# Latent attention of a six-block decoder on one core: lower context products with 66 stationary columns, each issued behind a turn

## The chip, the cores and the metric

The kernel runs on one core of one Trainium2 chip. The metric is device time in microseconds of a run. Lower is better.

## What is computed

The reference runs six blocks on x of 4 sequences x 256 tokens x 256 features, with a layer norm after each: sliding-window attention, cross attention to a context of 1601 rows x 64, a mixture of 8 experts, causal attention, the latent cross attention, and an attention with a second mixture of experts. The change lies in the fifth, the latent block. Per sequence b and head h (16 heads) it computes:

```
q_big = rope((hidden_q @ Wq.T) @ w_kc_q)
kv_r  = rope(kv_c)
scores = (q_big @ W_qr) . (kv_r @ W_kr)
attn  = softmax(scores)
ctx_c = attn @ kv_r
ctx   = ctx_c @ w_kc_kv.T
x    += ctx @ Wo.T
```

with kv_c the 1601 context rows. The kernel folds the weights of a head, so that a score is a product of the absorbed query with the roped context itself, and `ctx_c` is a 64-wide sum over 1601 rows.

## The kernel before

Most products are in two parts: a matrix is stored as an upper part rounded to fp32r and a lower part, the rest (names in `_hi` and `_lo`). `kvb[b]` holds for each of 13 tiles of 128 context rows the 64 features of `kv_r`: columns 0 to 63 the upper part, columns 64 to 127 the lower one. With that tile as the stationary operand, one product gives 128 rows: the sum over the upper part in rows 0 to 63, over the lower part in rows 64 to 127, and the weights of the output (`wf`) hold both halves.

`latent_attention` (L2427) goes through 64 units, one for each head and sequence. A unit consists of

- **absorb_q** (L2510), 6 products, after the query was projected (`project_q`, 12 products) and roped on POOL;
- **score** (L2521): for each half i of 128 queries, four pieces j of 304, 496, 496 and 305 context rows, in banks 0 to 3; two products each. A score waits until ACT's exponential has emptied the bank (`exped.at(s - 3)`, the piece four before it);
- **maximum** (L2692) on DVE, a reduction of each piece; after the fourth a small reduction, for which the exponential of the first piece waits;
- **exponential** (L2627) on ACT, with a read of the row sum, into `e_P`;
- **turn** (L2537) on PE: transposes of the probabilities, two tiles of context rows x two halves of queries in one of two banks; seven groups g (the last one has one tile of 65 rows), 26 transposes in a unit;
- **upper_pt** (L2641) on ACT, which copies the turned group to `e_PT_hi`, and **lower_pt** (L2709) on DVE, which takes the rest to `e_PT_lo`;
- **attend** (L2551) on PE: for each tile one product with `e_PT_hi` and one with `e_PT_lo`, all with the same stationary `kvb` tile, summed in one bank; 13 + 13 products in a unit. At g = 0 it waits for `cx_lo`, DVE's copy (L2717) of the previous unit's sum out of that bank;
- **project_out** (L2567), 6 products, and the addition to X on DVE.

All engines run the same loop of 8 steps for each unit (PE's at L2584), written out by hand, in the order of the code. While unit u is scored, unit u-1 is turned and summed: turn(v, step) at steps 0 to 6, attend(v, step-3) at steps 3 to 7 and attend(w, step+5), of the unit before, at steps 0 and 1. A step of PE is: four turns, up to four sums, one score of two products, then at step 1 absorb_q, at step 3 project_q, at step 5 the folding of a next head's weights, at step 7 project_out. A step of ACT is one exponential, copies for the step, upper_pt; of DVE one maximum and one lower_pt, with lower_context and lower_qk at step 2.

Of the kernel before, what the change touches and what calls it, by code (L numbers as in the profile page):

```python
# [16 lines left out]
P = 128  # L17
BATCH, SEQ, D = 4, 256, 256
TILES = BATCH * SEQ // P
DC = D // P  # L20
CTX, LAT = 1601, 64
# [33 lines left out]
def decoder(nc, t, out):  # L55
    with ExitStack() as top:
        pe, act, dve, pool, sp = nc.tensor, nc.scalar, nc.vector, nc.gpsimd, nc.sync
# [20 lines left out]
        bank = [psum[:, i, :] for i in range(8)]  # L78

        ident = vec("ident", [P, P])  # L80
# [18 lines left out]
        def mm(o, a, b, start, stop):  # L99
            return pe.matmul(o, a, b, start=start, stop=stop, skip_group_check=True)  # L100
# [2326 lines left out]
        def latent_attention(latent, before, following):  # L2427
            H, HALFQ = 16, latent.HALFQ
            LAG = 3
            PT_BUFS = LAG + 1  # L2430


            PIECES = (304, 496, 496, CTX - 1296)
# [2 lines left out]
            GROUPS = -(-KT // 2)  # L2436
            score_bank, tb_bank, ctx_bank, aux = (0, 1, 2, 3), (4, 5), 6, 7
# [5 lines left out]
            with ExitStack() as sc:  # L2443
# [27 lines left out]
                def keys_of(g):  # L2471

                    return min(2, KT - 2 * g), min(P, CTX - 2 * g * P)
# [12 lines left out]
                def tensor():  # L2486
                    free = [None]

                    def aux_bank():
                        if free[0]:  # L2490
                            pe.wait_ge(*free[0])
                        return bank[aux]

                    def fold_q(h):
                        latent.fold_q(h, aux_bank())
                        free[0] = wq_lo.at(h + 1)

                    def fold_r(h):
                        latent.fold_r(h, aux_bank())
                        free[0] = w2_lo.at(h + 1)  # L2500

                    def fold_o(h):
                        latent.fold_o(h, aux_bank())
                        free[0] = wf_lo.at(h + 1)

                    def project_q(m):
                        latent.project_q(m, aux_bank())
                        free[0] = q_kept.at(m + 1)

                    def absorb_q(m):  # L2510
                        h, z = m // BATCH, qr[m % 2]
                        pe.wait_ge(*z_lo.at(m + 1))
                        pe.wait_ge(*w2_lo.at(h + 1))
                        o = aux_bank()
                        for c in range(2):
                            last = mm3(o[:, 0:SEQ], [x[:, c, :] for x in w2[h % 2]], (z[0][:, c, :], z[1][:, c, :]),
                                       c == 0, c == 1)
                        last.then_inc(*q_absorbed.up())
                        free[0] = qk_lo.at(m + 1)

                    def score(u, i, j):  # L2521
                        s, k, o = 8 * u + 4 * i + j, qk[u % 2], bank[score_bank[j]]
                        if i == 0 and j == 0:
                            pe.wait_ge(*qk_lo.at(u + 1))
                            if u == 0:
                                pe.wait_ge(*latent.k_kept.at(latent.QUADS * BATCH + 1))
                                pe.wait_ge(*latent.padded.at(1))
                                pe.wait_ge(*q_kept.at(2))
                        if s >= 4:
                            pe.wait_ge(*exped.at(s - 3))  # L2530
                        size = PIECES[j] + PIECES[j] % 2
                        for n in range(2):
                            last = mm(o[:, 0:size], k[n][:, i * P:(i + 1) * P],
                                      KTb[:, u % BATCH, STARTS[j]:STARTS[j] + size], n == 0, n == 1)
                        last.then_inc(*scored.up())

                    def turn(u, g):  # L2537
                        at, p = GROUPS * u + g, Pm[u % 2]
                        o = bank[tb_bank[at % 2]]
                        n, rows = keys_of(g)  # L2540
                        pe.wait_ge(*exped.at(8 * u + 8))
                        if at >= 2:
                            pe.wait_ge(*pt_lo.at(at - 1))
                        for c in range(n):
                            k0 = (2 * g + c) * P
                            for i in range(2):
                                last = pe.transpose(o[0:rows, c * SEQ + i * P:c * SEQ + (i + 1) * P],  # L2547
                                                    p[:, i, k0:k0 + rows], ident[:])
                        last.then_inc(*turned.up())

                    def attend(u, g):  # L2551
                        at = GROUPS * u + g
                        x = PT[at % PT_BUFS]
                        n, rows = keys_of(g)
                        if g == 0:
                            if u == 0:
                                pe.wait_ge(*latent.kv_lo.at(BATCH))
                            else:
                                pe.wait_ge(*cx_lo.at(u))
                        pe.wait_ge(*pt_lo.at(at + 1))  # L2560
                        for c in range(n):
                            for y in range(2):
                                last = mm(bank[ctx_bank][:, 0:SEQ], kvb[u % BATCH][0:rows, 2 * g + c, :], x[y][0:rows, c, :],
                                          g == 0 and c == 0 and y == 0, g == GROUPS - 1 and c == n - 1 and y == 1)
                        last.then_inc(*attended.up())

                    def project_out(u):  # L2567
                        h, c = u // BATCH, cx[u % 2]
                        pe.wait_ge(*cx_lo.at(u + 1))
                        pe.wait_ge(*wf_lo.at(h + 1))  # L2570
                        o = aux_bank()
                        for i in range(2):
                            rows = slice(i * P, (i + 1) * P)
                            last = mm3(o[:, i * D:(i + 1) * D], (c[0][:, rows], c[1][:, rows]), [x[:] for x in wf[h % 2]],
                                       True, True)
                        last.then_inc(*put_out.up())
                        free[0] = x_added.at(u + 1)

                    pe.wait_ge(*before)
                    absorb_q(0)  # L2580
                    for j in range(4):
                        score(0, 0, j)
                    fold_o(0)
                    for i in range(N + 3):  # L2584
                        u, v, w, after = a_unit(i), a_unit(i - 1), a_unit(i - 2), a_unit(i + 1)
                        h, quarter = i // BATCH + 1, i % BATCH
                        for step in range(8):
                            half, j = divmod(step, 4)
                            if v is not None and step < GROUPS:
                                turn(v, step)  # L2590
                            if step == 2 and i == N:
                                enter_tensor(0, enter_bank)
                            if step < LAG and w is not None and step - LAG + 8 < GROUPS:
                                attend(w, step - LAG + 8)
                            if step >= LAG and v is not None:
                                attend(v, step - LAG)
                            if half == 0 and u is not None:
                                score(u, 1, j)
                            elif half == 1 and after is not None:
                                score(after, 0, j)  # L2600
                            if step == 1 and after is not None:
                                absorb_q(after)
                            if step == 3 and i + 2 < N:
                                if i + 2 == BATCH - 1:
                                    aux_bank()
                                    norm_tensor(12 + BATCH - 1, BATCH - 1, aux)
                                    free[0] = (xt_lo, 12 + BATCH)
                                project_q(i + 2)
                            if step == 5 and h < H and quarter < 3:
                                (fold_q, fold_r, fold_o)[quarter](h)  # L2610
                            if step == 7 and w is not None:
                                project_out(w)
# [350 lines left out]
```

## Time and profile before

| | |
|---|---|
| median of 3 runs | 1926.72 us |
| lowest, highest | 1924.54, 1929.82 us |
| span of the profiled execution, first to last instruction | 1919.4 us |
| mean granted TensorE clock | 0.979 |
| PE, PEld busy | 93%, 78% |
| DVE, ACT, POOL busy | 67%, 57%, 36% |

PE is the matmul engine and PEld its weight loads, which overlap the matmuls; DVE is VectorE, ACT ScalarE, POOL GpSimd. The run's own time of the profiled execution isn't given apart; its span lies 7.3 us under the median, 5.1 us under the lowest run. The latent stage reaches from about 790 to 1630 us of the span. Records of matmuls overlap: each is 0.27 to 0.5 us long, while the next begins 0.11 us or more after it, so the distance of two starts is what a matmul takes of the engine.

### The profile page before, as it was taken

The numbers are of one execution on the slowest core, as the hardware profiler recorded it, in microseconds if no ns is written. First come the engines' busy times: TensorE is split into PE (matmuls) and PEld (weight loads), VectorE is DVE, ScalarE is ACT, GpSimd is POOL, SyncE is SP. The second block draws the span as 40 slices with busy tenths as digits, with TensorE's granted clock in tenths as the row PEclk, the third lists the DMA queues.
The fourth block names the chain that finished last, engine by engine and source line by source line (L and its number), as shares of the span: only waits on it lengthen the run. The fifth ranks groups of instructions, "written<-read, shape, count | busy, mean of one in ns | idle before, by whom it ended". The sixth has DMA issues, their size and how long they took to land.

```text
span 1919.4 us, 42082 instructions
## 1 busy us (share of the span) xinstructions
PE 1791.9 (93%) x15752; PEld 1490.5 (78%) x15752; DVE 1282.1 (67%) x3335; ACT 1088.8 (57%) x2750; POOL 686.3 (36%) x674
## 2 busy tenths in 40 slices
PE   7999998889998998699999999999999998898995
PEld 6999977646656776599999999999999997674663
DVE  5676657742237666488888888888888888775222
ACT  4766654312213333488888888888888885531221
POOL 5643322132223532344433444344433441123221
PEclk8999999989999999899999999999999999999998
DMA  4000019222328000000000000000000001402223
GB/s 165 23 2 1 1 55 359 69 93 45 45 54 266 11 3 2 22 12 12 12 12 12 28 12 12 12 12 12 12 2 12 1 2 72 204 2 81 46 47 66
DMA packets 51861, 91.69 MB, mean 48 GB/s; under 512 B 4592, under 2 KB 43632, under 8 KB 49232
## 3 DMA queue, kind: packets, MB, share of 16 engines
q1 hardware_dynamic: 42928, 78.16, 12.1%
q0 software_dynamic: 8160, 10.29, 3.5%
q8 instruction: 130, 2.13, 0.5%
q10 hardware_dynamic: 576, 0.56, 0.1%
q14 instruction: 67, 0.55, 0.1%
HBM read 56.13 MB, written 32.87 MB: 46 GB/s over the span
## 4 chain that ended last, share of the span: by engine, by line
PE 77%; DVE 11%; ACT 6%; issue 2%; DMA 2%; POOL 2%; SPq 0%; DVEq 0%; ACTq 0%; POOLq 0%
PE bank L100 63%; PE bank L2547 10%; ACT d_PT L1339 2%; ACT landing L1339 2%; PE bank L1160 1%; PE bank L1888 1%; DVE a_t L707 1%; PE bank L505 1%; PE bank L1867 1%; DVE tiny L133 1%; DVE X L172 1%; DVE d_nm L1427 1%; DVE tiny L128 0%; DVE a_t L704 0%; DMA c_sums<-c_y,c_xs 0%
## 5 line engine op out<-in xcount | busy, mean ns | idle before, releaser
L2695 DVE TENSOR_REDUCE e_st<-bank 128x1 f32<-128x496 f32 (+2 forms) x512 | 291.6, 570 | 122.1 <-PE bank L100 121.0
L2632 ACT ACTIVATE e_P<-bank,e_st 128x496 f32<-128x496 f32 (+2 forms) x512 | 307.2, 600 | 94.5 <-DVE e_st L2699 92.9
L2714 DVE TENSOR_TENSOR e_PT_lo<-bank,e_PT_hi 128x512 fp32r<-128x512 f32 (+1 forms) x448 | 287.2, 641 | 1.5 <-ACT e_PT_hi L2647 1.4
L2547 PE MATMUL bank<-ident,e_P 128*128 128x128 f32 (+1 forms) x1664 | 258.3, 274 | 4.2 <-DVE e_PT_lo L2714 3.7
L2647 ACT CAST e_PT_hi<-bank 128x512 fp32r<-128x512 f32 (+1 forms) x448 | 248.5, 555 | 10.7 <-PE bank L2547 6.6
L100 PE MATMUL bank<-e_PT_hi,e_kv 128*128 128x256 f32 (+1 forms) x832 | 249.0, 320 | 0.0
L2547 PEld LDWEIGHTS bank<-ident,e_P 128*128 128x128 f32 (+1 forms) x1664 | 194.9, 140 | 31.0 <-issue 26.3
L100 PE MATMUL bank<-e_PT_lo,e_kv 128*128 128x256 f32 (+1 forms) x832 | 215.6, 279 | 0.0
L100 PE MATMUL bank<-e_KT,e_qk_hi 128*128 128x496 f32 (+2 forms) x512 | 199.0, 389 | 7.2 <-ACT e_P L2632 5.7
L100 PE MATMUL bank<-e_KT,e_qk_lo 128*128 128x496 f32 (+2 forms) x512 | 177.1, 346 | 0.0
L100 PEld LDWEIGHTS bank<-e_PT_lo,e_kv 128*128 128x128 f32 (+1 forms) x832 | 158.4, 190 | 2.4
L100 PEld LDWEIGHTS bank<-e_PT_hi,e_kv 128*128 128x128 f32 (+1 forms) x832 | 157.6, 189 | 2.2
L100 PE MATMUL bank<-mask_b,ident_b 128*128 128x128 bf16 (+2 forms) x924 | 132.5, 271 | 11.3 <-DVE d_nm L1429 6.8
L100 PEld LDWEIGHTS bank<-e_KT,e_qk_hi 128*128 128x128 f32 x512 | 95.9, 187 | 30.0 <-ACT e_P L2632 20.3
L2394 POOL TENSOR_TENSOR e_r<-x_in,e_ropeq 96x512 f32<-96x512 f32 x32 | 40.9, 1279 | 217.6 <-ACT x_in L2315 217.6
L2394 POOL TENSOR_TENSOR x_in<-x_in,e_ropeq 96x512 f32<-96x512 f32 x32 | 41.0, 1281 | 205.0 <-ACT x_in L2315 205.0
L100 PEld LDWEIGHTS bank<-mask_b,ident_b 128*128 128x128 bf16 x924 | 71.0, 99 | 49.8 <-DVE d_nm L1429 8.5
L2632 ACT ACTIVATION_READ_ACCUMULATOR e_P<-bank,e_st 128x1 f32 x512 | 102.6, 200 | 0.0
L1532 POOL TENSOR_SCALAR_AFFINE_SELECT landing<-landing 128x768 f32<-128x768 f32 x64 | 39.5, 642 | 168.4 <-ACT landing L1339 168.4
L100 PEld LDWEIGHTS bank<-e_KT,e_qk_lo 128*128 128x128 f32 x512 | 96.9, 189 | 0.1
L1339 ACT ACTIVATE d_PT<-bank 128x1536 f32<-128x1536 f32 x32 | 46.5, 1452 | 86.6 <-PE bank L100 86.6
L1339 ACT ACTIVATE landing<-bank 128x1536 f32<-128x1536 f32 x32 | 46.4, 1451 | 81.4 <-PE bank L100 81.4
(470 smaller groups left out, 4955.9 us busy)
## 6 DMA issues: line engine op xcount, KB each, us to landing
c_wall<-in_c_w SPq DMA_DIRECT2D x8, 1536.0 KB, 18.9
g_wall<-in_g_w SPq DMA_DIRECT2D x8, 1536.0 KB, 19.1
c_rows<-normed SPq DMA_DIRECT2D x9, 1040.0 KB, 12.8
g_rows<-normed SPq DMA_DIRECT2D x9, 1040.0 KB, 13.5
e_stage<-in_e_w SPq DMA_DIRECT2D x16, 416.0 KB, 3.2
c_xs<-c_rows SPq DMA_DIRECT2D x23, 130.0 KB, 2.1
g_xs<-g_rows SPq DMA_DIRECT2D x23, 130.0 KB, 2.1
landing<-in_a_wo SPq DMA_DIRECT2D x2, 1024.0 KB, 6.0
```

The lines of the kernel that those rows point to most:

```text
L100: return pe.matmul(o, a, b, start=start, stop=stop, skip_group_check=True)
L133: stats = dve.bn_stats(T[:, 6 * i:6 * i + 6], X[:, 2 * b + i, :])
L172: normed = dve.tensor_scalar(X[:, 2 * b + i, :], X[:, 2 * b + i, :], T[:, 12 + 2 * i:13 + 2 * i], T[:, 18 + i:19 + i], ALU.subtract, ALU.mult)
L505: last = pe.transpose(o[:, r * P:(r + 1) * P], p[:, r * P:(r + 1) * P], ident[:])
L1339: act.activation(PT[n % 2].rearrange("p a j n -> p (a j n)"), psum[:, B_BANK:B_BANK + 3, :].rearrange("p a n -> p (a n)"), ACT.Exp, scale= ...
L1532: last = pool.affine_select(blocks, blocks, pattern=pattern, compare_op=ALU.is_ge, fill=0.0, base=0, channel_multiplier=-1)
L2394: pool.tensor_tensor(x1, v, self.ropeq[:, 0:2, :], ALU.mult)
L2547: last = pe.transpose(o[0:rows, c * SEQ + i * P:c * SEQ + (i + 1) * P], p[:, i, k0:k0 + rows], ident[:])
L2632: act.activation(Pm[u % 2][:, i, STARTS[j]:STARTS[j] + n], bank[score_bank[j]][:, 0:n], ACT.Exp, bias=s[:, i, 4:5], accum_out=s[:, i, j:j ...
L2647: act.copy(PT[at % PT_BUFS][0][0:rows, 0:n, :], bank[tb_bank[at % 2]][0:rows, 0:n * SEQ].rearrange("p (c n) -> p c n", c=n)).then_inc(*pt_ ...
L2695: last = dve.tensor_reduce(s[:, i, j:j + 1], bank[score_bank[j]][:, 0:PIECES[j]], AX.X, ALU.max)
L2714: dve.tensor_tensor(lo, bank[tb_bank[at % 2]][0:rows, 0:n * SEQ].rearrange("p (c n) -> p c n", c=n), hi.bitcast(F32), ALU.subtract).then_i ...
```

## The change

The lower products (`e_PT_lo`) take 66 of the 128 columns of the `kvb` tile and write rows 0 to 65 of the bank. The lower part of the probabilities with columns 66 to 127 of the tile is no longer multiplied. Turns and sums of a step are woven into each other: turn, upper product, turn, lower product, and again for the second tile; where a step has only two turns (step 6), each stands between an upper and a lower product. The waits of the two old functions stand in `turn_ready` and `attend_ready`.

```diff
--- before.py
+++ after.py
@@ -2428,6 +2428,7 @@
             H, HALFQ = 16, latent.HALFQ
             LAG = 3
             PT_BUFS = LAG + 1
+            NARROW = LAT + 2
 
 
             PIECES = (304, 496, 496, CTX - 1296)
@@ -2534,35 +2535,62 @@
                                       KTb[:, u % BATCH, STARTS[j]:STARTS[j] + size], n == 0, n == 1)
                         last.then_inc(*scored.up())
 
-                    def turn(u, g):
-                        at, p = GROUPS * u + g, Pm[u % 2]
-                        o = bank[tb_bank[at % 2]]
-                        n, rows = keys_of(g)
+                    def turn_ready(u, g):
+                        at = GROUPS * u + g
                         pe.wait_ge(*exped.at(8 * u + 8))
                         if at >= 2:
                             pe.wait_ge(*pt_lo.at(at - 1))
-                        for c in range(n):
-                            k0 = (2 * g + c) * P
-                            for i in range(2):
-                                last = pe.transpose(o[0:rows, c * SEQ + i * P:c * SEQ + (i + 1) * P],
-                                                    p[:, i, k0:k0 + rows], ident[:])
-                        last.then_inc(*turned.up())
-
-                    def attend(u, g):
-                        at = GROUPS * u + g
-                        x = PT[at % PT_BUFS]
+
+                    def turn_one(u, g, c, i):
+                        o, p = bank[tb_bank[(GROUPS * u + g) % 2]], Pm[u % 2]
                         n, rows = keys_of(g)
+                        k0 = (2 * g + c) * P
+                        last = pe.transpose(o[0:rows, c * SEQ + i * P:c * SEQ + (i + 1) * P], p[:, i, k0:k0 + rows], ident[:])
+                        if c == n - 1 and i == 1:
+                            last.then_inc(*turned.up())
+
+                    def attend_ready(u, g):
                         if g == 0:
                             if u == 0:
                                 pe.wait_ge(*latent.kv_lo.at(BATCH))
                             else:
                                 pe.wait_ge(*cx_lo.at(u))
-                        pe.wait_ge(*pt_lo.at(at + 1))
-                        for c in range(n):
-                            for y in range(2):
-                                last = mm(bank[ctx_bank][:, 0:SEQ], kvb[u % BATCH][0:rows, 2 * g + c, :], x[y][0:rows, c, :],
-                                          g == 0 and c == 0 and y == 0, g == GROUPS - 1 and c == n - 1 and y == 1)
-                        last.then_inc(*attended.up())
+                        pe.wait_ge(*pt_lo.at(GROUPS * u + g + 1))
+
+                    def attend_upper(u, g, c):
+                        n, rows = keys_of(g)
+                        x = PT[(GROUPS * u + g) % PT_BUFS][0]
+                        mm(bank[ctx_bank][:, 0:SEQ], kvb[u % BATCH][0:rows, 2 * g + c, :], x[0:rows, c, :],
+                           g == 0 and c == 0, False)
+
+                    def attend_lower(u, g, c):
+
+                        n, rows = keys_of(g)
+                        x = PT[(GROUPS * u + g) % PT_BUFS][1]
+                        last = mm(bank[ctx_bank][0:NARROW, 0:SEQ], kvb[u % BATCH][0:rows, 2 * g + c, 0:NARROW], x[0:rows, c, :],
+                                  False, g == GROUPS - 1 and c == n - 1)
+                        if c == n - 1:
+                            last.then_inc(*attended.up())
+
+                    def turn_and_attend(u, g, v, k):
+
+                        turns = [(c, i) for c in range(keys_of(g)[0]) for i in range(2)] if u is not None else []
+                        sums = range(keys_of(k)[0]) if v is not None else []
+                        if turns:
+                            turn_ready(u, g)
+                        for c in range(2):
+                            if c < len(sums):
+                                if len(turns) == 4:
+                                    turn_one(u, g, c, 0)
+                                if c == 0:
+                                    attend_ready(v, k)
+                                attend_upper(v, k, c)
+                                if turns:
+                                    turn_one(u, g, *turns[c if len(turns) == 2 else 2 * c + 1])
+                                attend_lower(v, k, c)
+                            elif turns:
+                                for at in turns[len(turns) // 2 * c:len(turns) // 2 * (c + 1)]:
+                                    turn_one(u, g, *at)
 
                     def project_out(u):
                         h, c = u // BATCH, cx[u % 2]
@@ -2586,14 +2614,10 @@
                         h, quarter = i // BATCH + 1, i % BATCH
                         for step in range(8):
                             half, j = divmod(step, 4)
-                            if v is not None and step < GROUPS:
-                                turn(v, step)
+                            y, k = (w, step - LAG + 8) if step < LAG else (v, step - LAG)
+                            turn_and_attend(v if step < GROUPS else None, step, y if k < GROUPS else None, k)
                             if step == 2 and i == N:
                                 enter_tensor(0, enter_bank)
-                            if step < LAG and w is not None and step - LAG + 8 < GROUPS:
-                                attend(w, step - LAG + 8)
-                            if step >= LAG and v is not None:
-                                attend(v, step - LAG)
                             if half == 0 and u is not None:
                                 score(u, 1, j)
                             elif half == 1 and after is not None:
```

The rows below are PE's, as the built programs have them; `ident,e_P` is a turn, `e_PT_hi,e_kv` an upper and `e_PT_lo,e_kv` a lower product, `e_KT,e_qk_hi` a score. The first number of a size is the stationary operand's columns, the second the moving columns. Step 3 before, up to the score (the following rows are project_q):

```order
L2547 MATMUL bank<-ident,e_P 128x128 x4
L100 MATMUL bank<-e_PT_hi,e_kv 128x256
L100 MATMUL bank<-e_PT_lo,e_kv 128x256
L100 MATMUL bank<-e_PT_hi,e_kv 128x256
L100 MATMUL bank<-e_PT_lo,e_kv 128x256
L100 MATMUL bank<-e_KT,e_qk_hi 128x306
```

and in the changed kernel; steps 0, 4 and 5 read the same:

```order
L2548 MATMUL bank<-ident,e_P 128x128
L100 MATMUL bank<-e_PT_hi,e_kv 128x256
L2548 MATMUL bank<-ident,e_P 128x128
L100 MATMUL bank<-e_PT_lo,e_kv 66x256
L2548 MATMUL bank<-ident,e_P 128x128
L100 MATMUL bank<-e_PT_hi,e_kv 128x256
L2548 MATMUL bank<-ident,e_P 128x128
L100 MATMUL bank<-e_PT_lo,e_kv 66x256
L100 MATMUL bank<-e_KT,e_qk_hi 128x306
```

The last turn, which tells ACT that the group is turned, stood behind three turns; it now stands behind three turns and three products. Step 6, with two turns of 65 columns, in the changed kernel:

```order
L100 MATMUL bank<-e_PT_hi,e_kv 128x256
L2548 MATMUL bank<-ident,e_P 65x128
L100 MATMUL bank<-e_PT_lo,e_kv 66x256
L100 MATMUL bank<-e_PT_hi,e_kv 128x256
L2548 MATMUL bank<-ident,e_P 65x128
L100 MATMUL bank<-e_PT_lo,e_kv 66x256
L100 MATMUL bank<-e_KT,e_qk_hi 128x496
```

Both turns stood ahead of the four products before. The orders of ACT, DVE and POOL are unchanged.

## Rows read from the trace of the kernel before

**Rows 1.** The page, part 1: busy time by engine.

```profile
PE 1791.9 (93%) x15752; PEld 1490.5 (78%) x15752; DVE 1282.1 (67%) x3335; ACT 1088.8 (57%) x2750; POOL 686.3 (36%) x674
```

**Rows 2.** Busy time in one stretch of the latent stage (windows).

```profile
1200.00:1400.00 200.00, 200.00 (x1492) 184.68 (x1491) 168.92 (x408) 163.31 (x439) 81.20 (x78) 1.00 0.04 11
```

**Rows 3.** Instructions that read or write e_PT_lo: duration, first and last start.

```profile
L100 PEld LDWEIGHTS bank<-e_PT_lo,e_kv x832: 187/189/338, 801.7 to 1615.0; 128*128 128x128 f32 x154, 65*128 65x128 f32 x13
```

**Rows 4.** Who waited for whom, 820 to 1600 us: total, times, longest.

```profile
ACT e_P L2632 <- DVE e_st L2699: 91.5, 107, 1.7
```

**Rows 5.** Groups by shape, whole span: busy us, mean ns.

```profile
L2547 PEld LDWEIGHTS bank<-ident,e_P 128*128 128x128 f32 x1536 | 180.1, 140 | 18.7 <-issue 18.1 <-ACT e_P L2632 0.4
...
L100 PEld LDWEIGHTS bank<-XT_lo,e_wq_hi 128*96 128x96 f32 x256 | 42.0, 164 | 0.1
```

**Rows 6.** PE in order of time, steps 0 to 6: start us, us.

```profile
1199.91 0.60 PE L2547 MATMUL bank<-ident,e_P 128*128 128x128 f32 x4
...
1200.47 0.28 PE L100 MATMUL bank<-e_PT_lo,e_kv 128*128 128x256 f32 x1
1200.59 0.28 PE L100 MATMUL bank<-e_PT_hi,e_kv 128*128 128x256 f32 x1
...
1205.55 0.28 PE L100 MATMUL bank<-XT_hi,e_wq_hi 128*96 128x256 f32 x1
1205.67 0.28 PE L100 MATMUL bank<-XT_lo,e_wq_hi 128*96 128x256 f32 x1
...
1206.96 0.60 PE L2547 MATMUL bank<-ident,e_P 128*128 128x128 f32 x4
...
1208.15 0.60 PE L2547 MATMUL bank<-ident,e_P 128*128 128x128 f32 x4
...
1209.52 0.81 PE L100 MATMUL bank<-e_stage 128*128 128x192 f32 x4
1210.17 0.38 PE L2547 MATMUL bank<-ident,e_P 128*65 128x128 f32 x2
```

**Rows 7.** PEld in order of time, same unit: start us, us.

```profile
1200.97 0.19 PEld L100 LDWEIGHTS bank<-e_KT,e_qk_hi 128*128 128x128 f32 x1 [0.19 <-ACT e_P L2632]
1201.07 0.19 PEld L100 LDWEIGHTS bank<-e_KT,e_qk_lo 128*128 128x128 f32 x1
...
1205.16 0.19 PEld L100 LDWEIGHTS bank<-e_KT,e_qk_hi 128*128 128x128 f32 x1
...
1208.95 0.19 PEld L100 LDWEIGHTS bank<-e_KT,e_qk_hi 128*128 128x128 f32 x1
...
1211.67 0.19 PEld L100 LDWEIGHTS bank<-e_KT,e_qk_hi 128*128 128x128 f32 x1
```

**Rows 8.** ACT in order of time, same unit.

```profile
1200.81 0.58 ACT L2647 CAST e_PT_hi<-bank 128x512 fp32r<-128x512 f32 x1
...
1204.90 0.20 ACT L2632 ACTIVATION_READ_ACCUMULATOR e_P<-bank,e_st 128x1 f32 x1
...
1207.64 0.58 ACT L2647 CAST e_PT_hi<-bank 128x512 fp32r<-128x512 f32 x1
...
1208.69 0.20 ACT L2632 ACTIVATION_READ_ACCUMULATOR e_P<-bank,e_st 128x1 f32 x1
1208.79 0.59 ACT L2647 CAST e_PT_hi<-bank 128x512 fp32r<-128x512 f32 x1
...
1210.74 0.37 ACT L2647 CAST e_PT_hi<-bank 65x256 fp32r<-65x256 f32 x1
...
1211.42 0.20 ACT L2632 ACTIVATION_READ_ACCUMULATOR e_P<-bank,e_st 128x1 f32 x1
```

**Rows 9.** DVE in order of time, same unit.

```profile
1204.05 0.41 DVE L2719 TENSOR_TENSOR e_cx_lo<-bank,e_cx_hi 128x256 fp32r<-128x256 f32 x1
```

**Rows 10.** ACT, then PEld, at the end of the following unit.

```profile
1224.24 0.20 ACT L2632 ACTIVATION_READ_ACCUMULATOR e_P<-bank,e_st 128x1 f32 x1
...
1224.64 0.19 PEld L100 LDWEIGHTS bank<-e_KT,e_qk_hi 128*128 128x128 f32 x1
```

## Prediction

> **What bounds the kernel now.** I read the page first: PE is busy 93% of the span, its weight loads (PEld) 78%, DVE 67% and ACT 57% [rows 1]. Those are averages over six blocks, so the second view is one stretch of the latent stage by itself: in 200 us PE is busy all of it at a granted clock of 1.00, DVE 168.92 us and ACT 163.31 us [rows 2]. The reader should distrust the 200: a matmul's record is 0.28 us long where the next one starts 0.12 us later [rows 6], so records cover pauses of 0.1 us and more. The third view, the lower products' own line, gives the stage its length: 832 of them from 801.7 to 1615.0 us, 813 us for 64 units, 12.7 us a unit [rows 3]. The waits show the coupling that the averages hide: ACT waits for DVE's small reduction 107 times, 91.5 us in all, in the 780 us of that view, which hold some 123 halves of a unit [rows 4]. So this is no stage with one full engine. It is a ring: score on PE, maximum on DVE, exponential on ACT, which frees the bank for a later score; and beside it, turn on PE, copy on ACT, lower part on DVE. In-order queues tie the two together. The last view is one unit in order of time on each engine [rows 6 to 9], where I look for which event stands directly behind which. All the sums below use that unit, in that execution, whose span of 1919.4 us lies 7.3 us under the median; I add the change to the median.
>
> **What the narrow operand can save.** A load of 128 columns takes 189 ns (median) [rows 3], one of 96 columns 164 ns [rows 5]: 25 ns for 32 columns, so about 0.05 us less for 62 columns fewer. That helps only where a load is longer than the matmul before it. Behind a product it isn't: products with 96-column weights start 0.12 us apart (1205.55, 1205.67), as those with 128 do (1200.47, 1200.59) [rows 6]. The change bets that it is so behind a turn. Four turns take 0.60 us and two take 0.38 us [rows 6]: 0.11 us for each turn more. A turn's load is already short, 140 ns [rows 5], and in the pair of 0.38 us it has 65 columns; the turns are 0.11 us apart all the same. So a short load behind a turn doesn't shorten it. The moving side explains it: four f32 products of 192 moving columns begin at 1209.52 and what follows them at 1210.17 [rows 6], 0.16 us each, 0.85 ns a column; a turn of 128 f32 columns by that rate takes 0.11 us. A turn therefore covers a full load of 128 columns (the second load of a score follows the first after 0.10 us [rows 7]). I take **nothing** for the narrow loads. The bounds are 0 and 0.05 us for each of the 11 lower products of a unit that get a turn ahead of them (steps 0, 1, 3, 4, 5 and 6: 2+1+2+2+2+2), 704 in all, 35 us.
>
> The Trainium skill speaks for the bet: "TensorE: Matmul & The Clock Gate", sections "Back-to-back issue gap" and "LDWEIGHTS (loading the stationary operand)", gives a warm matmul N/2.4 + 2.5 ns and a load P/1.2 ns. By that a turn of 128 columns would take 56 ns, a full load would stick out by half, and 66 columns would take 55 ns; the trace agrees on the slope of the load but not on the turn. What it would do here is the first rival.
>
> **What the weaving costs on PE itself.** Runs of turns per unit go from 7 to 22 (steps 0, 3, 4, 5: 4 each instead of 1; step 1: 3; step 2: 1; step 6: 2). The group of four turns begins at 1199.91 and the second product at 1200.47 [rows 6]: 0.56 = 4 x 0.11 + 0.12, so a change between turns and products costs 0.01 us or less. I take 0 to 0.01 for each of the 15 more, up to 0.15 us a unit. It is no more than the uncertainty of the following.
>
> **What the weaving delays.** The last turn of a step, which releases ACT's copy, now has three products of 0.12 ahead of it: it ends 0.36 us later after the step's begin, 0.37 with the changeovers. The products end when they did. Who waits for it, step by step, counting how much later than before each event comes:
>
> 1. Step 0. The turns end at 1200.51, ACT's copy starts at 1200.81. The wake takes 0.04 us (turns' end 1208.75, copy 1208.79 [rows 6, 8]), so 0.26 us of slack hide most: the copy, and with it the next exponential and score, come **0.11** later.
> 2. Step 3. The first product of a unit waits for cx_lo, which ends at 1204.46 [rows 9], now 1204.57. Before, the four turns were issued while PE waited for it. Now three of them stand behind that product in PE's queue. It streams after a wake of 0.06 (row sum's end 1205.10, load 1205.16 [rows 7, 8]) and a load of 0.10, at 1204.73; then four products (0.48) and three turns (0.34) bring the score to 1205.55, where before its load began at 1205.16 and its stream at 1205.26: **0.29** later.
> 3. Step 4. project_q follows that score without a pause, so the turns of step 4 begin 0.29 later and the last ends 0.66 later. Before they ended at 1207.56 and the copy began at 1207.64 [rows 6, 8], 0.04 beyond the wake. The copy comes **0.62** later, and the exponential behind it.
> 4. Steps 5 and 6. The score of step 5 waits for that exponential already (row sum's end 1208.89, load 1208.95 [rows 7, 8]), so PE is 0.62 late too. In step 6 the last of two turns began 0.11 after the step's begin; now an upper product, a turn, a lower and an upper one stand ahead of it, 0.47: 0.36 more. It ended at 1210.55, so now at 1211.53, and the copy begins at 1211.57 instead of 1210.74 [rows 6, 8]: **0.83** later. The last exponential follows.
> 5. Step 7. The fourth score waits for that exponential's row sum: end 1211.62, load 1211.67 [rows 7, 8], so it is 0.83 later and with it the next unit. In the following unit the distance is 0.20 (1224.44, 1224.64 [rows 10]), 0.14 of slack, which leaves 0.69. Mean of the two: 0.76 us.
>
> Copies and maxima on DVE move along; it was idle for 31 us of 200 [rows 2] and absorbs nothing of a chain that runs through ACT and PE. No DMA, no order on ACT, DVE or POOL changes. 63 rounds have both units in hand: 63 x 0.76 = **48 us**. 1926.7 + 48 = 1975 us. Its own bounds: if at step 6 nothing is added the round is 0.62, 39 us, 1966; if every round is like the first, with 0.15 for changeovers, 0.98, 62 us, 1988. A measurement of this kernel tells about 0.3% (6 us) from no change.
>
> **The rivals.**
> - *Loads do bind behind a turn and PE alone counts.* 704 x 0.05 = 35 us saved, less 960 changeovers at 0.01: 25 us, 1902. For it: PE is the busiest engine. Against: the 65-column turns at 0.11, and copies of ACT that start 0.08 and 0.04 us after the end of their turns. It decides if a lower product starts 0.06 us after a turn and ACT doesn't wait. Chance 0.07. It is also what the Trainium skill's "TensorE: Matmul & The Clock Gate" would have.
> - *Loads bind, and the last turn is late as well.* The woven step is 0.10 shorter, of which 0.05 ahead of the last turn: with 0.32 instead of 0.37 the chain gives 0.06, 0.14, 0.42, 0.73, and 0.66 with the slack of step 7: 63 x 0.66 = 42 us if the weaving saves nothing else on PE, 30 us if it saves what isn't waited for; 1963. Chance 0.12.
> - *The lateness hides.* ACT's queue may have more slack in most units than in the two I read: then only changeovers are left, 0 to 10 us, 1927 to 1937. Against it: the wakes of 0.04 to 0.06 us at steps 4, 5 and 7. Chance 0.08, half of it within 0.3%.
> - *A changeover with a single turn costs more than one with four.* The trace has no single turn. At 0.05 instead of 0.01 on the path, 15 x 0.05 x 63 = 47 us more: 2022. Chance 0.05.
>
> **How the numbers follow.** The chain has 0.68. The range of 1948 to 1998 holds it with 10 us at its high end for what a second copy in the chain adds, and the second rival, with 18 us below the chain's lower bound for units that differ from the two read; it leaves out the first rival, the third and the fourth, together 0.20. Faster by over 0.3%: 0.07. Within: 0.04. Slower: 0.89.
>
> **What the profile after should show.** A lower product's load at about 140 ns, yet the lower product 0.11 us after the turn. Unit length 13.4 to 13.5 us, the lower products over 860 us instead of 813. ACT idle ahead of its e_PT_hi copies with PE's turn as the releaser, in place of almost none; the first product of step 3 with a turn waiting behind it. The forecast is wrong in its first step if products follow turns after 0.06 us, in its second if the stage is longer but ACT doesn't wait for turns.

## The result, and the profile after

| | before | changed |
|---|---|---|
| median | 1927.63 us (4 runs, 1924.54 to 1929.82) | 1969.84 us (4 runs, 1967.56 to 1971.13) |
| ratio | | 1.0217, 95% interval 1.0203 to 1.0232 |
| span of the profiled execution | 1919.4 us | 1969.1 us |
| first to last lower product | 801.7 to 1615.0, 813.3 us | 800.8 to 1661.3, 860.5 us |

The change costs 42 us by the medians. In the two profiled executions the latent stage grew by 47.2 us and the span by 49.7.

Page, part 1, of the changed kernel, as [rows 1] of before:

```profile
PE 1832.6 (93%) x15752; PEld 1499.5 (76%) x15752; DVE 1287.9 (65%) x3335; ACT 1112.9 (57%) x2750; POOL 685.2 (35%) x674
```

PE's busy time rose by 41 us and its share didn't move; nothing here says why. The same stretch of the stage as [rows 2] (PE, PEld, DVE, ACT, POOL busy of 200 us, clock, DMA share, GB/s):

```profile
1200.00:1400.00 200.00, 197.28 (x1406) 175.81 (x1406) 161.50 (x385) 159.67 (x413) 78.38 (x75) 1.00 0.04 11
```

In the same 200 us there are 1406 matmuls instead of 1492, and every engine is less busy than before: a stage that got longer by waiting. The clock is 1.00 as before. The lower products, as [rows 3] (durations of their loads, first and last start):

```profile
L100 PEld LDWEIGHTS bank<-e_PT_lo,e_kv x832: 135/138/229, 800.8 to 1661.3; 128*66 128x66 f32 x154, 65*66 65x66 f32 x13
```

The load of 66 columns has a median of 138 ns instead of 189: the narrow operand did to the load what it should. Waits from 820 to 1600 us, the window of [rows 4] (who waited for whom, us in total, times, longest), of the changed kernel:

```profile
ACT e_P L2656 <- DVE e_st L2723: 72.6, 116, 0.9
PEld bank L100 <- ACT e_P L2656: 46.8, 159, 0.8
ACT e_PT_hi L2671 <- PE bank L2548: 45.7, 149, 0.4
```

and the last two of them in the kernel before, same window:

```profile
PEld bank L100 <- ACT e_P L2632: 12.8, 62, 0.9
ACT e_PT_hi L2647 <- PE bank L2547: 0.4, 1, 0.4
```

ACT's copies of turned groups now wait 149 times for PE's turns, where they waited once before. PEld's wait for the exponential went from 12.8 to 46.8 us; I read it as the same delay come round.

One unit in order of time (start us, us), the same kind of unit as [rows 6 to 9] show of before. PE, then its loads, then ACT, then DVE:

```profile
1222.23 0.27 PE L2548 MATMUL bank<-ident,e_P 128*128 128x128 f32 x1
...
1222.92 0.27 PE L2548 MATMUL bank<-ident,e_P 128*128 128x128 f32 x1
...
1229.57 0.27 PE L2548 MATMUL bank<-ident,e_P 128*128 128x128 f32 x1
1229.59 0.37 PE L100 MATMUL bank<-e_PT_hi,e_kv 128*128 128x256 f32 x1
1229.80 0.27 PE L2548 MATMUL bank<-ident,e_P 128*128 128x128 f32 x1
1229.82 0.36 PE L100 MATMUL bank<-e_PT_lo,e_kv 128*66 128x256 f32 x1
1230.02 0.27 PE L2548 MATMUL bank<-ident,e_P 128*128 128x128 f32 x1
1230.05 0.37 PE L100 MATMUL bank<-e_PT_hi,e_kv 128*128 128x256 f32 x1
1230.26 0.27 PE L2548 MATMUL bank<-ident,e_P 128*128 128x128 f32 x1
```

```profile
1226.96 0.19 PEld L100 LDWEIGHTS bank<-e_PT_hi,e_kv 128*128 128x128 f32 x1
...
1227.76 0.19 PEld L100 LDWEIGHTS bank<-e_KT,e_qk_hi 128*128 128x128 f32 x1
1227.88 0.19 PEld L100 LDWEIGHTS bank<-e_KT,e_qk_lo 128*128 128x128 f32 x1
...
1231.87 0.19 PEld L100 LDWEIGHTS bank<-e_KT,e_qk_hi 128*128 128x128 f32 x1 [0.27 <-ACT e_P L2656]
...
1234.76 0.19 PEld L100 LDWEIGHTS bank<-e_KT,e_qk_hi 128*128 128x128 f32 x1 [0.17 <-ACT e_P L2656]
```

```profile
1223.22 0.59 ACT L2671 CAST e_PT_hi<-bank 128x512 fp32r<-128x512 f32 x1
...
1230.57 0.59 ACT L2671 CAST e_PT_hi<-bank 128x512 fp32r<-128x512 f32 x1 [0.22 <-PE bank L2548]
...
1231.62 0.20 ACT L2656 ACTIVATION_READ_ACCUMULATOR e_P<-bank,e_st 128x1 f32 x1
...
1233.84 0.37 ACT L2671 CAST e_PT_hi<-bank 65x256 fp32r<-65x256 f32 x1
...
1234.52 0.20 ACT L2656 ACTIVATION_READ_ACCUMULATOR e_P<-bank,e_st 128x1 f32 x1
```

```profile
1226.47 0.41 DVE L2743 TENSOR_TENSOR e_cx_lo<-bank,e_cx_hi 128x256 fp32r<-128x256 f32 x1
```

In PE's rows look at the turns of step 4, at 1229.57, 1229.80 and 1230.02: a turn and an upper product take 0.23 us, a turn and a lower product of 66 columns 0.22. (The product's record starts 0.02 us after the turn's, while runs of one kind are 0.11 us and more apart; so only the sum of the two is read here.)

### The profile page after: what moved, and what is told of

It is laid out like the page before. It is cut to its first block, busy times and chain, and to the rows that moved or that the text cites. A ratio compares the mean times of both kernels' runs of the same rounds, so it can differ in the third digit from the quotient of the medians.

```text
span 1969.1 us, 42082 instructions
## 1 busy us (share of the span) xinstructions
PE 1832.6 (93%) x15752; PEld 1499.5 (76%) x15752; DVE 1287.9 (65%) x3335; ACT 1112.9 (57%) x2750; POOL 685.2 (35%) x674
## 3 DMA queue, kind: packets, MB, share of 16 engines
q1 hardware_dynamic: 42928, 78.16, 11.8%
## 4 chain that ended last, share of the span: by engine, by line
PE 74%; DVE 9%; ACT 8%; issue 5%; DMA 2%; POOL 2%; SPq 0%; ACTq 0%; DVEq 0%; POOLq 0%
PE bank L100 62%; PE bank L2548 8%; ACT e_P L2656 3%; ACT d_PT L1339 2%; ACT landing L1339 1%; PE bank L1888 1%; PE bank L1160 1%; DVE a_t L707 1%; PE bank L505 1%; PE bank L1867 1%; POOL c_rows L1768 1%; DVE d_nm L1427 0%; DVE X L172 0%; DVE a_t L704 0%; DMA g_sums<-g_y,g_xs 0%
## 5 line engine op out<-in xcount | busy, mean ns | idle before, releaser
L2548 PE MATMUL bank<-ident,e_P 128*128 128x128 f32 (+1 forms) x1664 | 379.3, 274 | 1.7 <-DVE e_PT_lo L2738 1.1
L100 PE MATMUL bank<-e_PT_hi,e_kv 128*128 128x256 f32 (+1 forms) x832 | 287.6, 349 | 2.6 <-ACT e_P L2656 2.1
L100 PE MATMUL bank<-e_PT_lo,e_kv 128*66 128x256 f32 (+1 forms) x832 | 286.8, 350 | 0.0
L2548 PEld LDWEIGHTS bank<-ident,e_P 128*128 128x128 f32 (+1 forms) x1664 | 226.5, 141 | 19.7 <-issue 17.9
L100 PE MATMUL bank<-e_KT,e_qk_hi 128*128 128x496 f32 (+2 forms) x512 | 210.1, 410 | 17.6 <-ACT e_P L2656 13.3
L100 PEld LDWEIGHTS bank<-e_PT_lo,e_kv 128*66 128x66 f32 (+1 forms) x832 | 115.0, 138 | 2.3
```

## The experiments

The length of the stage below is the time from the first to the last lower product's load; it leaves out the other five blocks. The rest of the span differs between executions: in the eleven profiled ones the span less the stage runs from 1106.1 to 1115.3 us. A stage is that of one profiled execution. Each ratio is against the kernel before run again beside the experiment (medians 1926.83 us for experiments 1 to 4, 1922.56 for 5 to 7, 1929.23 for 8 and 9). The lower products have 66 columns in all but one, so the lower probabilities with the lower part of the tile are left out in these as in the change. The name e5 in a forecast is experiment 5.

**1. The narrow operand alone**

```diff
 order of the steps as before
-mm(bank[ctx_bank][:, 0:SEQ], kvb[..][0:rows, .., :], x[1]..)
+mm(bank[ctx_bank][0:66, 0:SEQ], kvb[..][0:rows, .., 0:66], x[1]..)
```

> The order of the kernel before, the lower products with 66 columns (the lower probabilities with the tile's lower part are left out, as in the change). Chain theory (turns that end late hold ACT's copies): nothing, within 3 us of the kernel before, since no event moves and a load behind a product is hidden at 96 or 128 columns. A theory in which the 66-column products themselves cost something (a form that drains or loads badly) expects a good part of the 42 us here: 1940 or more.

Measured: 1925.89 us, ratio 0.9993 (0.9979 to 1.0006).

```profile
L100 PEld LDWEIGHTS bank<-e_PT_lo,e_kv x832: 135/138/232, 803.5 to 1618.3; 128*66 128x66 f32 x154, 65*66 65x66 f32 x13
```

A stage of 814.8 us against 813.3, with loads 51 ns shorter. The shorter load is worth nothing where it stands behind a product, and the narrow product costs at most 1 us by the interval.

**2. The weaving alone**

```diff
-            NARROW = LAT + 2
+            NARROW = P
```

on the changed kernel.

> The weaving of the change with all 128 columns in the lower products. Chain theory: within 4 us of the changed kernel, 1970, since a turn takes 0.11 us and covers a full load, so the narrow operand gave nothing. Load theory (a full load sticks out behind a turn, 0.05 us for 704 products, and the change lost in spite of that saving): up to 35 us slower than the changed kernel, 2005. In the profile a lower product starts as long after its turn as an upper one by the first theory and as with 66 columns.

Measured: 1975.56 us, ratio 1.025 (1.0231 to 1.0269), against 1.0217 for the change, with an interval that touches it. The stage is the better measure here:

```profile
L100 PEld LDWEIGHTS bank<-e_PT_lo,e_kv x832: 187/189/331, 801.4 to 1662.2; 128*128 128x128 f32 x154, 65*128 65x128 f32 x13
```

860.8 us, against 860.5 of the changed kernel. The median of 1975.56 lies 1.6 us outside what I expected, but this stage doesn't, and load theory allowed up to 35 us more in it. The profiled execution was the fastest of its four (1968.61 us, the others 1975 to 1976). Its span outside the stage is 1106.6 us, near the low end of those seen, which by itself leaves room for such a difference; no stage of the slower three is on record. A turn, a lower product with 128 columns and the next turn, in PE's order of time:

```profile
1223.03 0.27 PE L2550 MATMUL bank<-ident,e_P 128*128 128x128 f32 x1
1223.05 0.37 PE L100 MATMUL bank<-e_PT_lo,e_kv 128*128 128x256 f32 x1
1223.26 0.27 PE L2550 MATMUL bank<-ident,e_P 128*128 128x128 f32 x1
```

The two turns are 0.23 us apart. The median of all 321 such places of the stage is 0.23 us, and it is 0.23 us in the changed kernel with 66 columns too. So a load of 128 columns fits behind a turn, and the whole loss is the weaving's.

**3 and 4. The same weaving at one step only**

```diff
+            WOVEN = (4,)        # experiment 3;  (5,) in experiment 4
 turn_and_attend(u, g, v, k):
+    if g not in WOVEN: turns first, then the sums, as before
```

> 66 columns, only step 4 of each unit woven (3 more runs of turns a unit). Chain theory: the last turn of step 4 ends 0.37 us later, 0.04 of it hidden, so the exponential and the score of step 5 come 0.33 later, and with 0 to 0.14 slack at step 7 a round gets 0.26 longer on the mean: 16 us, 1944, bounds 12 to 21 us. Changeover theory (the loss is 15 more runs of turns at 0.044 us each): 3 x 64 x 0.044 = 8 us, 1936.

> 66 columns, only step 5 woven: the same 3 more runs of turns and the same 0.37 us of lateness as at step 4, but behind it stands an exponential whose bank is asked for 0.7 us later. Chain theory: hidden, 0 to 5 us, 1927 to 1932. Changeover theory: 8 us as at step 4, 1936. A difference between this and step 4 speaks for the chain.

Measured: step 4 1945.34 us, ratio 1.0084 (1.0057 to 1.0111); step 5 1932.22 us, ratio 1.0031 (1.0015 to 1.0047). The lower products of step 4 only and of step 5 only, and what ACT's copies waited for turns in each from 820 to 1600 us:

```profile
L100 PEld LDWEIGHTS bank<-e_PT_lo,e_kv x832: 135/138/232, 803.4 to 1635.7; 128*66 128x66 f32 x154, 65*66 65x66 f32 x13
```

```profile
L100 PEld LDWEIGHTS bank<-e_PT_lo,e_kv x832: 135/138/232, 800.3 to 1618.9; 128*66 128x66 f32 x154, 65*66 65x66 f32 x13
```

```profile
ACT e_PT_hi L2685 <- PE bank L2550: 13.1, 60, 0.2
```

```profile
ACT e_PT_hi L2685 <- PE bank L2550: 16.3, 61, 0.4
```

The stages are 832.3 and 818.6 us: 19.0 and 5.3 over the kernel before, for the same four instructions moved in the same way. ACT waited no less for turns where it cost less (16.3 us against 13.1). A wait of an engine's queue is no measure of a loss: behind the copy of step 4 stands an exponential that PE's next score already waits for, behind that of step 5 one that is asked for 0.7 us later. In the unit read of the kernel before, these are the end of that exponential's row sum, at 1210.04, and the load of the score of step 6:

```profile
1209.84 0.20 ACT L2632 ACTIVATION_READ_ACCUMULATOR e_P<-bank,e_st 128x1 f32 x1
```

```profile
1210.74 0.19 PEld L100 LDWEIGHTS bank<-e_KT,e_qk_hi 128*128 128x128 f32 x1
```

A price for each changeover, the rival, would have given both the same.

The 5.3 us at step 5 are at the edge of what I allowed, and the trace shows where they are. Of the 0.70 us of slack above, 0.65 are the four folding products of step 5 (1209.52 to 1210.17 [rows 6]). PE has such products in three units of four, and none for the last head. Counting a round from a unit's first turn to the next unit's, and leaving out the last two rounds, in which the stage runs out, 44 rounds have folding products, and with step 5 woven they are 0.02 us longer than before (median), 0.9 us in all. The 17 without them are 0.24 us longer, 4.2 us in all. So the same move hides where another product fills the time and costs where none does; both units that the prediction read have folding products.

**5. Late turns without more changeovers**

```diff
-turn turn turn turn  upper lower  upper lower
+upper lower  turn turn turn turn  upper lower
```

at steps 0, 3, 4 and 5.

> 66 columns; at steps 0, 3, 4 and 5 an upper and a lower product, then the four turns in one run, then the other two products. The number of runs of turns is that of the kernel before; the last turn ends 0.24 us later. Chain theory: step 0 hidden (slack 0.26); at step 3 the first product waits for cx_lo and the turns behind it, the score comes 0.28 later; at step 4 0.24 more less 0.04 of slack, 0.48; less 0.07 at step 7, so 0.41 to 0.48 a round, 26 to 30 us: 1955. Changeover theory: nothing, 1927, since no changeover is added.

Measured: 1961.56 us, ratio 1.0194 (1.0165 to 1.0223).

```profile
L100 PEld LDWEIGHTS bank<-e_PT_lo,e_kv x832: 135/140/199, 805.3 to 1657.3; 128*66 128x66 f32 x154, 65*66 65x66 f32 x13
```

A stage of 852.0 us, 38.7 over the kernel before. With as many runs of turns as before, the changeover theory expected none of it. But it is also more than my 26 to 30. The trace shows where: cx_lo, and the loads of the first product behind it and of the score that ends the step:

```profile
1226.95 0.41 DVE L2757 TENSOR_TENSOR e_cx_lo<-bank,e_cx_hi 128x256 fp32r<-128x256 f32 x1
```

```profile
1227.59 0.19 PEld L100 LDWEIGHTS bank<-e_PT_hi,e_kv 128*128 128x128 f32 x1 [0.68 <-issue]
...
1228.49 0.19 PEld L100 LDWEIGHTS bank<-e_KT,e_qk_hi 128*128 128x128 f32 x1
```

cx_lo ends at 1227.36, the load starts at 1227.59, 0.23 us later, as in the other units (median of 63: 0.227); the changed kernel's starts at 1226.96 after an end at 1226.88, 0.08 us in this unit and 0.053 in the median. I had reckoned with 0.06. Experiments 8 and 9 go after this.

**6 and 7. One step unwoven**

```diff
+            WOVEN = (0, 1, 2, 3, 4, 5)     # experiment 6;  (0, 1, 2, 4, 5, 6) in experiment 7
```

> The changed kernel with step 6 unwoven. Chain theory: what reached 0.62 at step 5 goes on as 0.62 to the last exponential, less 0 to 0.14 of slack at step 7: 0.55 a round instead of 0.76, 35 us over the kernel before instead of 48 by the same working, so 7 to 13 us under the changed kernel: 1960. Changeover theory: one run of turns fewer a unit, 3 us under it: 1967.

> The changed kernel with step 3 unwoven, so that the four turns run again while PE waits for cx_lo. Chain theory: at the score of step 3 0.11 is left of 0.29, the rest of the chain is unchanged, 0.58 instead of 0.76: 10 to 12 us under the changed kernel, 1959. Changeover theory: three runs of turns fewer a unit, 3 x 64 x 0.044 = 8 us: 1962. This run tells the two apart less than the others; it measures the term of step 3.

Measured: 1958.75 us, ratio 1.0183 (1.0154 to 1.0212), and 1960.77 us, ratio 1.0191 (1.0162 to 1.022).

```profile
L100 PEld LDWEIGHTS bank<-e_PT_lo,e_kv x832: 135/138/143, 805.1 to 1653.4; 128*66 128x66 f32 x154, 65*66 65x66 f32 x13
```

```profile
L100 PEld LDWEIGHTS bank<-e_PT_lo,e_kv x832: 135/138/143, 802.6 to 1651.3; 128*66 128x66 f32 x154, 65*66 65x66 f32 x13
```

Stages of 848.3 and 848.7 us, 12.2 and 11.8 under the changed kernel. Step 6 was to give back 7 to 13, step 3 10 to 12. Step 6 adds one run of turns, step 3 three; they cost the same, as by the chain and not as by a price for each run. The medians say less: they are 36 and 38 us over the kernel before, against 42 for the change, each with an interval of about 6 us to either side, so what they give back is 4 to 6 us and not clear of noise. The 12 us rest on the stage of one execution each.

**8. Experiment 5 without its step 3**

> e5_pair_first with step 3 in the order of the kernel before, so the pair of products stands ahead of the turns at steps 0, 4 and 5 alone. The stage, from the first to the last lower product, is 813.3 us before and 852.0 us in e5. Chain theory: step 0 hidden; step 4 0.24 less 0.04 of slack, 0.20 to the exponential; less 0.05 to 0.14 at step 7: 0.06 to 0.15 a round, 4 to 10 us, a stage of 817 to 823 us. Then step 3 alone was worth 29 to 35 us in e5. If the pair ahead costs the same at each of its four steps, a quarter of the 38.7 us goes: 842 us.

Measured: 1939.62 us, ratio 1.0053 (1.0034 to 1.0072).

```profile
L100 PEld LDWEIGHTS bank<-e_PT_lo,e_kv x832: 135/140/232, 804.9 to 1629.8; 128*66 128x66 f32 x154, 65*66 65x66 f32 x13
```

A stage of 824.9 us, 11.6 over the kernel before, a little above the 4 to 10 expected; so step 3 was 27 of the 38.7 us, just under the 29 to 35 that went with that.

**9. Experiment 5 with the waits apart**

```diff
-turn_ready(u, g)
 attend_ready(v, k)
 upper, lower
+turn_ready(u, g)
 turn, turn, turn, turn
```

> e5_pair_first with the turns' waits issued behind the pair of products instead of ahead of it, so that the first product of step 3 has only its own waits ahead. In e5 its load starts 0.23 us after cx_lo ends, in the changed kernel 0.08 us after. Theory that PE's queue takes waits one after the other when they are released late: the load comes 0.08 to 0.15 us after cx_lo, and 63 x 0.08 to 0.15 = 5 to 9 us go: a stage of 843 to 847 us. Theory that the excess of e5 over its forecast (38.7 against 26 to 30) has another cause: 852 us as in e5.

Measured: 1956.71 us, ratio 1.0147 (1.0119 to 1.0175).

```profile
L100 PEld LDWEIGHTS bank<-e_PT_lo,e_kv x832: 135/140/231, 802.7 to 1644.4; 128*66 128x66 f32 x154, 65*66 65x66 f32 x13
```

```profile
1218.98 0.41 DVE L2757 TENSOR_TENSOR e_cx_lo<-bank,e_cx_hi 128x256 fp32r<-128x256 f32 x1
```

```profile
1219.45 0.19 PEld L100 LDWEIGHTS bank<-e_PT_hi,e_kv 128*128 128x128 f32 x1 [0.51 <-DVE e_cx_lo L2757]
```

The load starts at 1219.45, 0.05 us after cx_lo's end at 1219.39 (median of 63 units 0.053), and the stage is 841.7 us, 10.3 less than in experiment 5 and 1.3 under the 843 to 847 expected. 63 x (0.23 - 0.05) = 11. The excess of experiment 5 was this: the turns' waits and the product's own stood in a row in PE's queue. Both traces have the waits that PE's queue took as separate instructions. In experiment 5 the one on cx_lo comes 0.04 us after cx_lo ends, another on DVE's lower parts at 0.15 and the load at 0.23 (medians of 63 units); in experiment 9 the load itself carries the wait on cx_lo.

No version of these beats the kernel before, and none points to one: in every order tried, a product that was moved ahead of a turn cost time or gave nothing.

## Why the prediction was right

The predicted 1975 us lie 5 us above the measured 1969.8, inside the range; the 48 us forecast for the stage compare with 47.2 in its profile. Step by step, how much later than before an event came, both counted from the first turn of the unit (1199.91 before, 1222.23 after, so 22.32 between them):

| event | before [rows 6 to 8] | after | later, predicted | later, measured |
|---|---|---|---|---|
| last turn of step 0 ends | 1200.51 | 1223.19 | 0.37 | 0.36 |
| its copy starts | 1200.81 | 1223.22 | 0.11 | 0.09 |
| load of the score of step 3 | 1205.16 | 1227.76 | 0.29 | 0.28 |
| copy of step 4 | 1207.64 | 1230.57 | 0.62 | 0.61 |
| row sum's end, step 5 | 1208.89 | 1231.82 | 0.62 | 0.61 |
| copy of step 6 | 1210.74 | 1233.84 | 0.83 | 0.78 |
| load of the score of step 7 | 1211.67 | 1234.76 | 0.83 | 0.77 |

- **The narrow operand gives nothing.** Right, shown by experiments 1 and 2. The argument from the 65-column turns and from the f32 products held: the turn's own 0.11 us covers a full load.
The Trainium skill, "TensorE: Matmul & The Clock Gate", section "Back-to-back issue gap", gives an isolated matmul N/2.4 + 2.5 ns, so a turn of 128 columns 56 ns, which is less than its load of 128 columns takes; it says itself that the formula leaves out the load. The 0.11 us from turn to turn in a run, with loads of 128 and of 65 columns alike [rows 6], and the same 0.23 us around a lower product of 66 and of 128 columns disagree, and the measurement decides.
- **Changeovers cost 0 to 0.01 us.** Right as far as it can be read: a turn and a product take 0.22 to 0.23 us [turns at 1229.57, 1229.80, 1230.02], and 0.11 + 0.12 was the sum of the two in their own runs. Experiments 4, 5, 6 and 7 exclude a price for each run as the cause of the loss.
- **Late turns hold ACT's copies.** Right in mechanism and size. The slack of 0.26 us at step 0 and 0.04 at step 4 was used up: the copies of steps 0 and 4 start 0.03 and 0.04 us after their turns end (1223.19 to 1223.22; of step 4, last turn 1230.26 + 0.27 = 1230.53 to 1230.57, 0.04).
- **Steps 6 and 7, and the mean.** Here the sizes were off in both units, in opposite directions. In the unit of the table the copy of step 6 comes 0.78 later instead of 0.83, and the score of step 7 0.77. In the following unit (its first turn is 23.09 us later than before) 0.69 was forecast for the score of step 7; its load, 1224.64 before [rows 10], comes 0.81 later. The slack of 0.14 there was used up as forecast, but the copy of step 6, at 1223.57 before, came 0.95 later:

```profile
1223.57 0.37 ACT L2647 CAST e_PT_hi<-bank 65x256 fp32r<-65x256 f32 x1
```

```profile
1247.61 0.37 ACT L2671 CAST e_PT_hi<-bank 65x256 fp32r<-65x256 f32 x1 [0.40 <-PE bank L2548]
...
1248.54 0.19 PEld L100 LDWEIGHTS bank<-e_KT,e_qk_hi 128*128 128x128 f32 x1 [0.17 <-ACT e_P L2656]
```

Over the stage's 63 rounds the median growth is 0.76 us, and all but the first two and the last two rounds lie between 0.58 and 0.86. So the chain acts in every unit. That the forecast mean of 0.76 meets this median is in part luck: the two units that it was made of were forecast at 0.83 and 0.69 and measured 0.77 and 0.81.
- **The rivals.** That loads bind is excluded by experiment 2. That the lateness hides is what step 5 does by itself (5.3 us for 16.3 us of ACT's waiting), but not the whole. Single turns at 0.05 us more would show in the 0.23 us and don't.

Open: the medians moved by 42 us, the stage of the profiled executions by 47. The profiled execution of before (span 1919.4) was faster than each of the runs shown; the kernel of experiment 1, whose stage is only 1.5 us longer, has a span of 1927.6 and a median of 1925.89, so a good part of such differences lies outside the stage. The 9 us between the least and the largest rest of a span cover the 5 us; which part of them is the stage's own isn't settled by these runs. Steps 0 and 1 were not woven or unwoven by themselves either: what they add (0.10 us to cx_lo in the unit read) is only seen with the others.

## What to carry to other kernels

Before filling the short slot behind an instruction, check from two rows whose operands differ that the slot is short: here runs of turns with 65 and with 128 stationary columns had the same pace, which told that the moving side sets it. And where the last instruction of a group releases another engine, what is put inside the group is paid by that engine if it has no slack there: order inside a step isn't free, even when the engine's own work doesn't grow. Read the slack at each release, since the same move cost 19 us at one step and 5 at the next, and in every kind of round, since 4 of the 5 came from the rounds without folding products.

## What the runs showed of the hardware that I had not expected

When PE's queue stood at a product behind several waits, the time from the last release to the load was 0.23 us (experiment 5: the turns' two waits and the product's own two ahead of it). It was 0.05 us in experiment 9, with only the product's own waits, and in the changed kernel, where a turn stands between the two pairs of waits (medians of 63 units). Splitting the waits so that each stands at the instruction that needs it gave 10 us back in 64 units.
